# Routed expert slots inside the steps of the attention phase, and layer-norm means taken out of the weights

## What is computed

```python
x = x + attention(layernorm(x), ctx)         # x, ctx: (128, 128, 256); linear attention, 16 heads
#   qp = elu(q) + 1, kp = elu(k) + 1; causal sums of kp * v, read by qp,
#   divided by the running sum of qp; then the product with Wo, plus bo
x = x + experts(layernorm(x))
#   h = relu(x @ W1 + b1); logits = h @ W2 + b2    (256 -> 128 -> 8 experts)
#   sel = argmax(logits)
#   out = x @ expert_W[sel] + expert_b[sel]        (8 matrices 256 x 256)
```

## Time and profile before

| | us |
|---|---|
| median of 3 runs (1157.48 to 1160.72) | 1159.31 |
| the profiled execution, its span | 1158.5 |
| TensorE matmuls busy | 1044.3 |
| VectorE busy | 843.8 |
| ScalarE busy | 562.7 |
| POOL busy | 587.0 |

### The profile page before, as it was taken

How to read it: one execution, slowest core, us unless ns; L and a number is a source line. 1 busy time by engine, 2 the same in 40 slices (tenths; PEclk the granted TensorE clock), 3 DMA queues, 4 the chain that set the end, 5 groups by cost and what they waited for, 6 DMA issues and landing times.

```text
span 1158.5 us, 39374 instructions
## 1 busy us (share of the span) xinstructions
PE 1044.3 (90%) x15828; PEld 727.5 (63%) x15829; DVE 843.8 (73%) x1739; ACT 562.7 (49%) x945; POOL 587.0 (51%) x682
## 2 busy tenths in 40 slices
PE   2989999999999999999999999999999626999996
PEld 1666666666666666666667666666667414666664
DVE  2688887887888887878878788888877643555554
ACT  2544544454555544554455545445444114666664
POOL 4144444544444455554555444544444444777766
PEclk9989999999999999999999999999999857999999
DMA  3823333333333333333334333333322014666664
GB/s 104 241 75 93 94 93 94 93 93 93 94 93 95 97 97 97 101 101 100 107 104 120 97 93 93 93 93 93 93 76 76 30 51 138 193 190 184 195 185 135
DMA packets 88601, 127.11 MB, mean 110 GB/s; under 512 B 13693, under 2 KB 67584, under 8 KB 88320
## 3 DMA queue, kind: packets, MB, share of 16 engines
q1 hardware_dynamic: 75392, 89.98, 30.1%
q0 software_dynamic: 13056, 34.90, 7.9%
HBM read 73.03 MB, written 36.06 MB: 94 GB/s over the span
## 4 chain that ended last, share of the span: by engine, by line
PE 23%; issue 23%; POOL 18%; DMA 13%; SPq 7%; ACT 5%; DVE 4%; DVEq 0%; POOLq 0%; ACTq 0%
DMA x_res<-in_x 8%; PE b_a L808 8%; POOL buckets L409 7%; PE b_b L1014 6%; SPq L338 5%; POOL x_res L433 3%; DMA stage<-buckets 2%; DMA out<-stage 2%; PE b_b L855 2%; PE b_a L1005 2%; ACT x2n L494 2%; POOL row L419 2%; PE b_a L803 2%; PE b_b L813 2%; ACT x2T L506 1%
## 5 line engine op out<-in xcount | busy, mean ns | idle before, releaser
L581 DVE TENSOR_TENSOR stage<-b_s,causal 128x1024 f32<-128x1024 f32 x192 | 226.1, 1219 | 47.6 <-PE b_s L835 37.1
L461 POOL DMA_INDIRECT out<-stage x136 | 136.6, 1005 | 59.2 <-issue 30.2
L409 POOL DMA_INDIRECT buckets<-row,place x128 | 140.8, 1100 | 34.6 <-issue 34.6
L1014 PE MATMUL b_b<-we_sb,x3T 128*128 x544 | 150.5, 400 | 0.0
L808 PE MATMUL b_a<-xnT,wq_sb 128*128 128x512 f32 x256 | 128.0, 624 | 7.4 <-ACT x2T L506 5.1
L539 ACT ACTIVATE x3n<-stage 128x256 f32<-128x256 f32 x136 | 81.5, 599 | 88.4 <-DMA stage<-buckets 83.8
L813 PE MATMUL b_b<-wo_sb,attT 128*128 128x256 f32 x512 | 121.4, 391 | 2.4 <-DVE attT L681 2.4
L494 ACT ACTIVATE x2n<-row 128x256 f32<-128x256 f32 x128 | 66.5, 590 | 115.5 <-POOL row L425 115.5
L407 POOL TENSOR_TENSOR onehots<-onehots,onehot 128x32 bf16<-128x32 bf16 x32 | 7.8, 244 | 223.6 <-DVE place L614 223.6
L808 PE MATMUL b_a<-ctxT,wk_sb 128*128 128x512 f32 x256 | 118.4, 605 | 1.8 <-ACT pos L480 1.8
L813 PE MATMUL b_b<-wv_sb,ctxT 128*128 128x256 f32 x512 | 119.0, 385 | 0.0
(11 more groups left out here) (119 smaller groups left out, 1954.4 us busy)
## 6 DMA issues: line engine op xcount, KB each, us to landing
stage<-buckets SPq DMA_DIRECT2D x136, 130.0 KB, 2.2
x_in<-in_x SPq DMA_DIRECT2D x32, 512.0 KB, 5.1
ctxT<-in_ctx SPq DMA_DIRECT2D x32, 512.0 KB, 6.3
qsel<-qp SPq DMA_DIRECT2D x256, 64.0 KB
x_res<-in_x SPq DMA_DIRECT2D x32, 512.0 KB, 7.3
out<-stage POOLq DMA_INDIRECT x136
we_sb<-in_L_ffn_expert_W SPq DMA_DIRECT2D x8, 256.0 KB, 6.0
buckets<-row,place POOLq DMA_INDIRECT x128
```

The lines of the kernel that those rows point to most:

```text
L409: pool.indirect_dma_start(buckets, bass.IndirectOffsetOnAxis(place[:, slot(route), t:t + 1], 0), row[:, slot(route), t, :], None).then_inc ...
L461: pool.indirect_dma_start(out.rearrange("t p n -> (t p) n"), bass.IndirectOffsetOnAxis(rows2[:, r, TOKEN:TOKEN + 1].bitcast(U32), 0), sums ...
L581: dve.tensor_tensor(dst.rearrange("p g h s q -> p g (h s) q"), b_s[:, :, 256 * t:256 * t + 256].rearrange("p g (a q) -> p g a q", q=C), ca ...
L1014: last = pe.matmul(b_b[:, h, 0:D], x3T[:, h, P * k:P * k + P], we_sb[:, k, bass.ds(e, 1), :], start=(k == 0), stop=(k == KC - 1))
```

## The change

**Slots in the first phase.** The second phase's loop is gone. From step 10 on each step takes a quad of four slots (`slots_of(j)`): slots 0 to 99 in steps 10 to 34, slots 100 to 103 in step 35 at an earlier place (`extra_slots_of`), 104 to 107 in step 36; 28 slots in seven quads (`TAIL`) come behind the last step, the first of them (108 to 111) without waiting for the padding. A table of eight slots is made by VectorE in steps 9, 11, ... 35 from the counts so far (`whole_blocks`, `fill_table`; 14 tables), which names only blocks that are already full and in `buckets`; the last table, with the remaining 24 slots and the places of padding, comes in step 36. TensorE counts by four or eight further matmuls in `ranks`.

In TensorE's step the quad's turns stand behind the w1 product, two slots' products behind the second half of wq, two behind the last sums, ahead of the logits. The next step's first scores wait for the quad's sums. VectorE adds the bias ahead of attT, in place in the ring (13 buffers, now of their own), makes the table there too, and adds the products, scaled by rstd, between onehot and the second half of qp. POOL scatters the quad at the head of the next step; the scatters of rows to `buckets` move behind x_res + bias (in step 36 they stay first; in step 35 rstd comes ahead of the quad). SP loads the rows behind x_res. Padding is written by SP from registers, not by POOL's indirect scatters. Registers are loaded four at a time.

**Means out of the weights.** Mean subtraction of both layernorms is taken into Wq, W1 and the expert matrices: each column's mean over its 256 rows is subtracted from it once. For Wq and W1 TensorE makes the means and VectorE subtracts them before the first step; for the experts this is done in steps 5 to 8, two experts a step (`expert_means`, `centre`). So x2n and xn are x * rstd, slots are multiplied as they are and scaled by rstd after the product, and nr, shift and ScalarE's normalizing of slots fall away.

```diff
+    STEPS = NG + STAGES - 1
+    RING = 13
+    QUAD = 4
+    BATCH = 2 * QUAD
+    TABLE_STEPS = range(9, STEPS - 1, 2)
+    TABLES = len(TABLE_STEPS)
+    LAST = SLOTS - BATCH * TABLES
+    CAP_BLOCKS = CAP // P
     WEIGHTS = 16 * 14
...
+        quad_of = quads(TABLE_STEPS[0] + 1, STEPS - 1 - TABLE_STEPS[0], 0)
+        extra_of = {STEPS - 2: quad_of.pop(STEPS - 2)}
+        EARLY = quad_of[STEPS - 1][-1] + 1
+        TAIL = [range(q, q + QUAD) for q in range(EARLY, SLOTS, QUAD)]
+        spare_banks = {q[0] // QUAD for q in list(extra_of.values()) + TAIL[0::2]}
...
+            for at in range(first, SLOTS if table == TABLES else first + BATCH, QUAD):
+                held_values.extend(nc.values_load_multi_w_load_instructions(
...
+                    table = table_of(slots[0])
+                    routed = TABLE_STEPS[table] - STAGES
+                    sp.wait_ge(s_bucket[routed % 2], 16 * GT * (routed // 2 + 1))
+                    sp.wait_ge(s_bucket[1 - routed % 2], 16 * GT * ((routed + 1) // 2))
+                    sp.wait_ge(s_tab, TAB * table + TAB)
+                    load_table(mybir.EngineType.SP, table, first_rows)
+                for i in slots:
+                    r = i % RING
+                    if i >= RING:
+                        sp.wait_ge(s_outs[r], 16 * (i // RING))
...
                     sp.dma_start(x_res[:, slot(attend), :, :], of_x(attend)).then_inc(s_xr[slot(attend)], 16)
+                for quad in (extra_slots_of(j), slots_of(j)):
+                    load_slots(quad)
                 if norm:
...
+            schedule(step)
+
+            for quad in TAIL[:1]:
+                load_slots(quad)
+            sp.wait_ge(s_spare, 16)
+            sp.wait_ge(s_tab, TAB * TABLES + TAB)
+            pads = nc.values_load_multi_w_load_instructions(
+                pad_of[0:1, :], [mybir.EngineType.SP], min_val=0, max_val=SPARE - P,
+                skip_runtime_bounds_check_because="an expert's rows end within its part")[1]
+            for e in range(E):
+                sp.dma_start(buckets[bass.ds(pads[e], P), :], pad_row[:, :]).then_inc(s_pad, 16)
             for s in range(2):
...
+            load_table(mybir.EngineType.SP, TABLES, first_rows)
+            for quad in TAIL[1:]:
+                load_slots(quad)
...
+                pool.tensor_tensor(ve2[:, :], row[:, slot(merge), :, MEAN + 1], column(eps_col),
+                                   ALU.add).then_inc(s_ve2, 1)
+                pool.wait_ge(s_ve2, n(merge, k=1))
+                pool.tensor_tensor(row[:, slot(merge), :, RSTD], ve2[:, :], column(neg_half),
+                                   ALU.pow).then_inc(s_rstd2, 1)
+                pool.tensor_copy(row[:, slot(merge), :, TOKEN].bitcast(U32),
+                                 tokens[:, bass.ds(n(merge, GT), GT)]).then_inc(s_token, 1)
+
...
+                    if j == STEPS - 1:
+                        scatter_rows(route)
+                if merge and j == STEPS - 2:
+                    scale2(merge)
+                for quad in (extra_slots_of(j - 1), slots_of(j - 1)):
+                    scatter(quad)
+                if merge and j < STEPS - 2:
+                    scale2(merge)
                 if attend:
                     pool.wait_ge(s_zinv, n(attend, k=1))
                     pool.tensor_tensor(z[:, :], z[:, :], u[:, :], ALU.mult).then_inc(s_zprod, 1)
@@ -433,39 +474,25 @@
                     pool.tensor_tensor(x_res[:, slot(attend), :, :], x_res[:, slot(attend), :, :],
                                        bias_o[:, :].rearrange("p (o n) -> p o n", o=1).to_broadcast((P, GT, D)),
...
+                if route and j < STEPS - 1:
+                    scatter_rows(route)
...
+            def turn_out(slots):
+
+                for pair in range(len(slots) // 2):
+                    i = slots[2 * pair]
+                    act.wait_ge(s_x3Tp, i // 2 + 1)
+                    if i >= BATCH:
+                        act.wait_ge(s_prod, (i - BATCH) // 2 + 1)
+                    act.activation(x3T[:, i // QUAD % 2, 2 * pair:2 * pair + 2, :],
...
-                                       bias=row[:, slot(merge), t, SHIFT:SHIFT + 1],
...
+                turn_out(slots_of(j))
...
+            dve.tensor_tensor(wq_sb[:, :, :], wq_sb[:, :, :],
+                              b_s[:, 0, 0:D].rearrange("p (o n) -> p o n", o=1).to_broadcast((P, KC, D)),
+                              ALU.subtract).then_inc(s_cst, 1)
+            dve.wait_ge(s_wmean, 2)
+            dve.tensor_tensor(w1_sb[:, :, :], w1_sb[:, :, :],
+                              b_s[:, 1, 0:FF].rearrange("p (o n) -> p o n", o=1).to_broadcast((P, KC, FF)),
+                              ALU.subtract).then_inc(s_cst, 1)
...
+                made(dve.tensor_scalar(whole[:, :], whole[:, :], ROUND, -ROUND, ALU.add, ALU.add))
+                dve.wait_ge(s_tab, before_it + 2)
+                made(dve.tensor_tensor(free[:, :], whole[:, :], taken[:, 0:E], ALU.subtract))
+                made(dve.scalar_tensor_tensor(jump[:, :], taken[:, 1:E + 1], float(CAP_BLOCKS), whole[:, :],
...
+            def add_bias(slots):
+
+                if slots and slots[0] % BATCH == 0 and slots[0] <= BATCH * TABLES:
+                    load_table(mybir.EngineType.DVE, table_of(slots[0]), experts)
+                for i in slots:
+                    r = i % RING
+                    e = experts.pop(0)
+                    dve.wait_ge(s_x3Tp, i // 2 + 1)
+                    dve.tensor_tensor(rows2[:, r, 0:D], rows2[:, r, 0:D],
+                                      bias_e[:, bass.ds(e, 1), :].rearrange("p o n -> p (o n)"),
+                                      ALU.add).then_inc(s_biased, 1)
+
+            def add_products(slots):
+                for i in slots:
+                    r = i % RING
+                    dve.wait_ge(s_biased, i + 1)
+                    dve.wait_ge(s_prod, i // 2 + 1)
+                    dve.scalar_tensor_tensor(rows2[:, r, 0:D], product_at(i), rows2[:, r, RSTD:RSTD + 1],
+                                             rows2[:, r, 0:D], ALU.mult, ALU.add).then_inc(s_sums, 1)
+
+            def centre(pair):
+
+                dve.wait_ge(s_means, pair + 1)
+                dve.tensor_tensor(we_sb[:, :, 2 * pair:2 * pair + 2, :], we_sb[:, :, 2 * pair:2 * pair + 2, :],
+                                  b_s[:, 2, :].rearrange("p (o e n) -> p o e n", o=1, n=D).to_broadcast((P, KC, 2, D)),
+                                  ALU.subtract).then_inc(s_centred, 1)
+
...
+                    if j in TABLE_STEPS:
+                        whole_blocks(TABLE_STEPS.index(j), False)
+                    if j == STEPS - 1:
+                        whole_blocks(TABLES, True)
...
+                add_bias(slots_of(j))
+                if j in TABLE_STEPS:
+                    fill_table(TABLE_STEPS.index(j), False)
                 if attend:
...
+                add_products(slots_of(j))
                 if norm:
                     queries(norm, 1)
...
+                    last = pe.matmul(b_s[:, 2, :], average[:, :], we_sb[:, k, 2 * pair:2 * pair + 2, :],
+                                     start=(k == 0), stop=(k == KC - 1))
+                last.then_inc(s_means, 1)
...
+            def turn(slots):
+
+                for i in slots:
+                    r = i % RING
+                    pe.wait_ge(s_rows2[r], 16 * (i // RING) + 16)
+                    into, at = turned_at(i)
+                    for k in range(KC):
+                        last = pe.transpose(into[:, at + P * k:at + P * k + P], rows2[:, r, P * k:P * k + P], ident[:, :])
+                    if i % 2:
+                        last.then_inc(s_x3Tp, 1)
+
+            def multiply(slots):
+
+                for i in slots:
+                    if i % BATCH == 0 and i <= BATCH * TABLES:
+                        load_table(mybir.EngineType.PE, table_of(i), experts)
+                    e = experts.pop(0)
+                    if i % 2 == 0:
+                        pe.wait_ge(s_x3T, i // 2 + 1)
+                        if i >= BATCH:
+                            pe.wait_ge(s_sums, i - BATCH + 2 if i >= EARLY else i // QUAD * QUAD)
+                    for k in range(KC):
+                        last = pe.matmul(product_at(i), x3T[:, i // QUAD % 2, i % QUAD, P * k:P * k + P],
+                                         we_sb[:, k, bass.ds(e, 1), :], start=(k == 0), stop=(k == KC - 1))
+                    if i % 2:
+                        last.then_inc(s_prod, 1)
+
+            def ranks(last_group):
                 out_of = b_a[:, 1, 0:GT * E]
...
+                for at, hot in enumerate(counted):
+                    last = pe.matmul(b_a[:, 1, GT * E:GT * E + E], ones[:, :], hot, start=(at == 0),
+                                     stop=(at == len(counted) - 1))
...
+                    if slots_of(j - 1):
+                        pe.wait_ge(s_sums, slots_of(j - 1)[-1] + 1)
+                    if 5 <= j - 1 < 5 + E // 2:
```

(15 more changed lines are left out.)

421 lines of the change are left out of this document (183 added, 238 removed).

## The result

The changed kernel takes 1115.79 us (median of 4 runs, 1114.80 to 1119.13) against 1159.64 us before: a ratio of 0.9628, with a 95% interval from 0.9609 to 0.9647. That is 3.7% less, where 1.6% less (1140 us) was forecast. Repeated later beside other kernels, the same kernel gave 0.9634 and 0.9640. The profiled execution spans 1113.1 us.

A forecast was written before the change was run, and what follows sets the result against it. TensorE was taken to bound the first phase and POOL the second. 1158.5 us plus 129 up to the last place, less 148 at the end, plus 0.8, gave 1140 us; range 1120 to 1155, with A and E 1115 to 1164.

The forecast's parts named there:

- the chain from place to x2n: POOL and ScalarE, full steps: place 0.7 to 0.9 us later against 0.96 of nr and shift removed, so nothing.
- A: Rival: register loads hidden and the end without stalls, 10 us less in the steps, 10 in the end: 1120; chance 0.14.
- register loads: TensorE, 26 loads in 13 tables at 0.74 us: 19 us if all shows, half taken, 10 us.
- the quad itself: TensorE, steps 10 to 34: products and turns 1.13 us per slot, 4.5 a step, 113 us, all on the path.
- Steps 5 to 9: First phase before slots: expert means add 8 us in steps 5 to 8; the 0.86 us xnT wait goes, 4 less.
- the start: Before the first statistics: means of wq and w1, eight matmuls and two subtractions, add 3 us.
- The end: Behind the last place: 28 slots reach POOL at T + 25, all done at T + 67, 148 us less than before.
- a ring of 13: Row buffers at the end: landing 3.3, load 2.8, turn and products 5 make 11 us for eight slots, allowing POOL's pace.
- B: Rival, slower: VectorE's product additions take up to 0.67 us, place slips, TensorE waits in 25 steps: 1165; chance 0.13.
- C: Rival: VectorE's new additions with two SBUF inputs block POOL's scatters, 2.2 us a step, 55 in all: 1195; chance 0.04.
- D: Rival: rows or table come late behind x_res, TensorE waits 1 to 2 us in 25 steps: 1165 to 1190; chance 0.05.
- E: Rival: small stalls of 0.65 to 0.9 us in sum per step cancel the gain: 1156 to 1163; chance 0.06.

The follow-up runs named there:

- run 1: Kernel after with the shift of x2n put back on the chain (POOL makes nr and shift, x2n takes it as bias): 1135.47 us, ratio 0.9782.
- run 4: Kernel before with only the means taken out of Wq and W1, xn and x2n without bias, second phase kept: 1140.43 us, ratio 0.9830.
- run 6: Kernel after with TensorE's register loads doubled (dropped from the program, 1118.31 us), then eight loads per table instead of two: 1140.80 us, ratio 0.9851.
- runs 7 to 12: Kernel after with two tables fewer (1131.68 us), then tail variants: 108 to 111 first, SP registers early, pairs, 14 buffers, TensorE loads early (1115.68 to 1107.34 us).
- run 5: Kernel after with POOL's four row scatters put back at the head of its step, ahead of slot scatters and rstd: 1262.07 us, ratio 1.0882.
- run 3: Kernel after with POOL making nr and shift behind rstd and x2n waiting for them, without the bias: 1130.94 us, ratio 0.9755.

## Why the prediction was wrong in size

**Right.** What bounds the kernel; that nearly all of TensorE's slot work is added to the path; that VectorE, POOL and SP have room; that the slots' scatters take 1.0 us each; and the build of the end. The sign held, the range (1115 to 1164) held by 0.8 us only, the size did not: half of the gain was missing, and nearly all its errors fell on one side.

**The step that failed** is the one that put the chain from place to x2n at nothing: "Against the 0.8 that place loses, the chain stays: nothing." Three sizes in it were off, all to one side. Place comes 0.51 later, not 0.7 to 0.9, and POOL gets the next operation out 0.2 us sooner after it, so the loss is 0.3. The forecast had the two kinds of scatters "at the same price", which hid that: the fourth row scatter took 1.49 us, the fourth slot scatter takes 0.98, and 0.3 us of this is given back since the first one starts later behind place. The gain is 1.0 us of nr and shift, as said, and 0.37 us that the forecast did not see at all, the bias operand of four activations. Together 1.0 - 0.3 + 0.4 = 1.1 us, more than the 0.86 us that TensorE waited: the wait vanished, and 0.79 us a step with it. An estimate of 0.96 against 0.8 is a difference of two numbers, and what was left of it lay within what either could be off. It should have been a rival of its own with some chance, and A, the rival on that side, had a different cause.

The trace of before held the answer. TensorE waited in 26 of 28 full steps; step 23 is one of the two without the wait, and its period is 27.05 us, not 27.84. Here are POOL's and VectorE's lines of the kernel before, of step 23 first and then of step 24:

```profile
604.57 0.96 POOL L409 DMA_INDIRECT buckets<-row,place  x1 [0.30 <-issue]
604.95 0.66 DVE L633 SCALAR_TENSOR_TENSOR kp<-ex,pos 128x512 f32<-128x512 f32 x1
606.97 0.20 POOL L422 TENSOR_TENSOR nr<-row,neg_one 128x4 f32<-128x4 f32 x1
```

```profile
631.62 1.49 POOL L409 DMA_INDIRECT buckets<-row,place  x1 [0.31 <-issue]
631.63 0.66 DVE L633 SCALAR_TENSOR_TENSOR kp<-ex,pos 128x512 f32<-128x512 f32 x1
634.50 0.68 DVE L641 SCALAR_TENSOR_TENSOR kp<-ex,pos 128x512 f32<-128x512 f32 x1
634.56 0.68 POOL L422 TENSOR_TENSOR nr<-row,neg_one 128x4 f32<-128x4 f32 x1
```

In step 24, as in nearly all, VectorE's kp, with both operands in SBUF, starts together with the fourth scatter and again just ahead of nr; the scatter takes 0.53 us more than in step 23 and nr 0.48. These 1.0 us are the difference between a step with the wait and one without. So half of the "0.96 us of nr and shift" was a collision and not work, and the same 0.79 us a step could have been read off two rows. Moving kp alone in the kernel before was not tried.

**The working in numbers.** The last place came at 1041, not 1072. Over the 23 steps 10 to 32 the forecast was 23 x (4.52 + 0.1 + 0.4) = 115 us, measured were 731.2 - 639.6 = 91.6. The parts of the 24 us:
- the chain, 23 x 0.79 = 18.2 less (runs 1 and 4);
- register loads, 23 x 0.4 = 9.2 less: two loads lie under matmuls already issued (run 6). Half of them had been taken as exposed; rival A had this right;
- the quad itself, 31.41 - 27.18 = 4.23 us and not 4.52, 6.7 less;
- against these, 8.8 us of steps longer than 31.41, most of it the gaps with no releaser, which nothing in the forecast allowed for.

These come to 25.3 us. The rest is the counting matmuls, 0.13 us a step and not 0.1, and the one step of 27.05 us in the kernel before.

Up to step 9 another 6 us were gained. Steps 5 to 9 went as the forecast said (+4.0 us, forecast +4.2), but the start did not: the first turns come 2.1 us later, forecast 3, and yet the first ranks 2.9 us earlier. By 65 us TensorE had waited 0.83 us for attT in the kernel after and 2.40 in the kernel before, and the next 16 matmuls took 3.72 against 6.70 us, the latter at the lower clock (0.56 granted from 65 to 72 us). This is not the change's doing: the second control, the same program as the kernel after, waits 2.40 us there too and has its first ranks at 99.6 us, and the other traces of that program have them at 96.5 and 99.8. Up to 4 us of the start differ from one execution to the next.

**The end** was 72.1 us against 67. POOL took up the 28 slots at T + 24.2 (forecast 25) and ended them 38.9 us later (forecast 38); the span ended 9.0 us behind the last scatter and not 4. That is no landing: POOL has seen all of them 1.5 us behind the scatter, and then stands in a closing DRAIN, 7.09 us where the kernel before has 2.53. These are the two rows, the kernel after first:

```profile
L52 POOLq DRAIN  x1: 7092/7092/7092, 1105.8 to 1105.8; - x1
```

```profile
L44 POOLq DRAIN  x1: 2527/2527/2527, 1155.7 to 1155.7; - x1
```

It is 7.1 to 7.7 us in every variant of the kernel after and 2.53 in run 4; what it waits for is open. It is nearly all of the 5 us by which the end was missed. The forecast's remark that a ring of 13 allows this pace was too kind: the waits that it did not count (14.0 us) are there, as 8.4 us ahead of slot 108 and in pieces behind, and runs 7 to 12 show that taking one away only moves it, until the buffers are held for a shorter time.

**The rivals.** A named 1120, 4 us from the time, but by luck: its hidden loads gave 9.2 us, and its end without stalls did not come. B (place too late) has the right place and the wrong sign: its addition takes 0.476 us, near the low bound of 0.42. C, scatters blocked, did happen for the rows, off the path. Three rows of one step of the kernel after, in which POOL's addition and first scatter of rows run beside VectorE's scan, with two operands in SBUF:

```profile
535.98 2.86 POOL L474 TENSOR_TENSOR x_res<-x_res,bias_o 128x1024 f32<-128x1024 f32 x1 [3.16 <-DMA x_res<-in_x]
536.64 4.35 DVE L786 TENSOR_TENSOR_SCAN z<-carry,qp 128x1024 f32<-128x1024 f32 x1
539.01 2.87 POOL L444 DMA_INDIRECT buckets<-row,place  x1 [0.17 <-issue]
```

The scan takes 2.29 us in the median, the scatter 0.96 at its shortest, the addition 2.34. The scan ends 2.2 us behind the addition's end, the scatter 0.9 behind the scan's. By the rule of the Trainium skill that the forecast weighed (SBUF — State Buffer, section "SBUF: two separate sides"), a VectorE instruction with two SBUF inputs and a GpSimd one that reads SBUF lock each other out of a shared port, and the one that started first goes first; the trace agrees in kind, here and at kp in the kernel before. The 3.1 us that the Trainium skill gives there is for a scatter beside a copy; the longest scatter of the kernel after took 2.97 us. At the place where it would have hurt, the four slot scatters between place and rstd took 1.0 us each. The forecast's "masks from PSUM, as before" was not the whole of it: kp runs there too, in the kernel before together with the fourth scatter, in the kernel after from 0.5 us into the third, which it does not lengthen. D did not come: TensorE never waited for a slot's rows in steps 10 to 33. E did in part, as 8.8/23 = 0.4 us a step of gaps, but cancelled no gain.

**What stays open.** The gaps with no releaser in the late sums (0.6 to 2.3 us, four to six times, nearly all between 690 and 870 us in this order of work, and some 50 to 100 us later with two tables fewer). Behind 100 us they are absent, or rare, in the runs where TensorE pauses elsewhere in each step or second step (runs 1, 5 and the eight loads), though run 3, with pauses of 0.5 us, still has four. That points to something TensorE is supplied with and nearly outruns, such as its instructions. The traces bear this out in their DMA packets. The page of the kernel after has this queue:

```profile
q8 instruction: 127, 2.08, 0.8%
```

Its packets are of 16 KB, one about every 7 us. The 18 traces have 90 gaps of over 0.5 us in the sums; every one of them ends 2.2 to 2.6 us after the start of such a packet, whether the gap lasts 0.5 us or 2.3. The gaps therefore seem to end when instructions arrive; this is read off the times and was not tested. Packets at the same point of other steps cause no gap, and why just these steps have one is open; no run changed the supply.

## What to carry to other kernels

Where an engine is bound by its own work but for one short wait, ask what remains of that wait as carefully as of the work: here it was worth 19 us, nearly half of the change, and two uncertain numbers had been cancelled against each other. If a few steps lack the wait, look at what is different in them first. Small operands and operations count exactly where they stand on such a chain and nowhere else, so move work off it (behind x_res, off the head of POOL's step) before making work smaller. In a phase that streams through a ring of buffers, count how long each buffer is held, from its load to the landing of its store: removing a gap in front gives nothing until that time is shorter.

## What was not expected of the hardware

- An activation with a bias column took 590 ns for 128x256, one without 497 ns, in all 18 traces; a column of zeros costs the same as one of data.
- A load into TensorE's registers takes 0.3 to 0.34 us and is hidden beside issued matmuls up to 1.0 to 1.2 us in all; behind that, or where TensorE has nothing issued, it shows in full.
- A pause of 5.0 us cost 6.1: the next matmuls ran at a granted clock of 0.57 (run 5). The pauses of 0.86 us of run 1 cost no more than themselves.
- VectorE's scan of 128x1024 took 4.35 instead of 2.29 us, and a POOL scatter 2.87 instead of 0.96, when they ran beside each other or beside POOL's addition in SBUF. A scatter that VectorE's kp joined at its start took 1.49 us; one that kp joined 0.37 us later took 0.96.
- POOL's closing DRAIN took 7.09 us in the kernel after and 2.53 in the kernel before, behind the last landing that POOL waited for.
- All 90 gaps of over 0.5 us without a releaser in TensorE's sums ended 2.2 to 2.6 us after the start of a 16 KB packet of the instruction queue.
